# Perceiver block: the small attention steps between the products of the tail are regrouped

## What is computed

```
x = x + cross_attention(layernorm(x), ctx, ...)     # 32 heads of 128, 8 key heads
x = x + self_attention(layernorm(x), Wq, Wk, Wv, Wo)  # 32 heads of 32, 8 key heads, rope, causal
x = x + mix(layernorm(x), W_res, W_pre, W_post, ...)  # 4 streams, 50 Sinkhorn rounds, branch product
```

## Time and profile before

| what | value |
|---|---|
| median of 3 runs | 1107.49 us |
| the three runs | 1107.48, 1107.49 and 1110.83 us |
| profiled execution | span 1105.4 us; no other time of its own is given |
| PE busy | 1074.2 us (97% of the span) |
| DVE busy | 812.7 us (74%) |
| ACT busy | 482.0 us (44%) |
| POOL busy | 198.3 us (18%) |

### The profile page before, as it was taken

One profiled execution on the slowest core, in us unless ns is written; L12 is line 12 of the kernel. 1 busy time (PEld: TensorE's weight loads), 2 busy tenths in 40 slices (PEclk: granted clock), 3 DMA queues, 4 the chain that ended last, 5 costly groups with the idle time before them and its releaser, 6 DMA issues.

```text
span 1105.4 us, 17806 instructions
## 1 busy us (share of the span) xinstructions
PE 1074.2 (97%) x6380; PEld 902.4 (82%) x6380; DVE 812.7 (74%) x1942; ACT 482.0 (44%) x1033; POOL 198.3 (18%) x198
## 2 busy tenths in 40 slices
PE   6999999999999999999999999999999999999688
PEld 4888888788888888888888888888888878888467
DVE  5887667666667878776668877757536798758997
ACT  4544434444445446544444455434213334431417
POOL 2000000233223233333232230000001032140001
PEclk9999999999999999999999999999999999999889
DMA  9975775244543333244455312699935614000001
GB/s 238 174 200 126 159 161 146 51 110 110 114 99 87 76 76 70 62 94 109 97 107 114 76 34 58 136 215 242 213 63 105 109 24 76 2 14 1 1 1 77
DMA packets 184542, 111.29 MB, mean 101 GB/s; under 512 B 108040, under 2 KB 174472, under 8 KB 184480
## 3 DMA queue, kind: packets, MB, share of 16 engines
q1 hardware_dynamic: 182080, 109.17, 45.8%
q10 hardware_dynamic: 2400, 1.31, 0.5%
HBM read 90.98 MB, written 18.94 MB: 99 GB/s over the span
## 4 chain that ended last, share of the span: by engine, by line
PE 94%; DVE 3%; ACT 1%; DMA 1%; issue 0%; SPq 0%; DVEq 0%
PE ps L635 32%; PE ps L535 16%; PE ps L602 14%; PE ps L983 9%; PE ps L519 4%; PE ps L663 4%; PE ps L646 4%; PE ps L971 2%; PE ps L746 1%; PE ps L936 1%; DMA raw<-in_L_xattn_q_proj_w 1%; PE ps L879 1%; PE ps L1076 1%; PE ps L864 1%; PE ps L847 1%; PE ps L943 0%
## 5 line engine op out<-in xcount | busy, mean ns | idle before, releaser
L635 PE MATMUL ps<-wt,act 128*128 128x512 f32 x1536 | 381.0, 394 | 0.0
L635 PEld LDWEIGHTS ps<-wt,act 128*128 128x128 f32 x1536 | 278.1, 188 | 51.8 <-issue 0.4
L535 PE MATMUL ps<-wt,act 128*128 128x512 f32 x768 | 179.1, 394 | 1.4 <-ACT act L1109 1.0
L535 PEld LDWEIGHTS ps<-wt,act 128*128 128x128 f32 x768 | 145.0, 190 | 33.3 <-ACT wt L1114 3.4
L602 PE MATMUL ps<-act,wt 128*128 128x512 f32 x672 | 153.7, 390 | 0.0
L1114 ACT ACTIVATE wt<-raw 128x512 fp32r<-128x512 f32 x192 | 106.6, 625 | 95.6 <-PE ps L535 52.1
L602 PEld LDWEIGHTS ps<-act,wt 128*128 128x128 f32 x672 | 125.9, 188 | 26.0
L1565 DVE STREAM_TRANSPOSE raw<-raw 128x1024 f32<-128x1024 f32 x92 | 107.9, 1216 | 22.6 <-DMA raw<-in_L_xattn_o_proj_w 22.6
L983 PE MATMUL ps<-wt,act 128*128 128x512 f32 x480 | 121.5, 400 | 0.0
L1573 DVE TENSOR_TENSOR wt<-raw,wt 128x512 fp32r<-128x512 f32 x172 | 107.4, 682 | 15.9 <-ACT wt L1114 15.8
L2391 POOL TENSOR_TENSOR small<-small 128x4 f32<-128x4 f32 (+2 forms) x64 | 69.0, 1080 | 246.1 <-DVE small L1587 200.2
(11 more groups left out here) (178 smaller groups left out, 1274.4 us busy)
## 6 DMA issues: line engine op xcount, KB each, us to landing
xr<-in_ctx SPq DMA_DIRECT2D x64, 256.0 KB, 4.9
raw<-in_L_xattn_o_proj_w SPq DMA_DIRECT2D x32, 512.0 KB, 14.6
raw<-in_L_xattn_q_proj_w SPq DMA_DIRECT2D x28, 512.0 KB, 9.2
xr<-q_rows SPq DMA_DIRECT2D x16, 512.0 KB, 4.2
ot_hi<-spare SPq DMA_DIRECT2D x64, 128.0 KB, 2.0
act<-ot_hi SPq DMA_DIRECT2D x32, 256.0 KB, 9.4
q_rows<-G SPq DMA_DIRECT2D x28, 256.0 KB, 2.7
raw<-in_L_xattn_k_proj_w SPq DMA_DIRECT2D x8, 512.0 KB, 6.9
```

The lines of the kernel that those rows point to most:

```text
L535: mm = pe.matmul(banks[t], lhs(p == 2, c, t), wt[:, n_slot, int(p == 1), c, :], start=(acc_from and q == 0), stop=(acc_to and q == 3 * NC ...
L635: mm = pe.matmul(bank, src[int(p == 2)][:, c, kt * P:(kt + 1) * P], wt[:, slot, int(p == 1), c, :], start=(q == 0), stop=(q == 3 * NC - 1))
```

## The change

`scores2(b-1)`, `weigh2(b-3)` and `turn_probs2(b-2)` now stand in this order at the end of the block. The probabilities are turned into the upper halves of banks 2 to 5, beside the scores, no longer into banks 6 and 7. `turn_out2` moves to the next block, behind q = 8, and with it scale_out2, hi_out2 and lo_out2 go one block later. In the output projection the low activation parts of chunks 4 to 7 come last (`low_late`). ACT makes hi_out2 ahead of the weights' high parts, and copy_query ahead of exp2. DVE does scale_out2, rotate_query and lo_out2 ahead of read, peak and centre. `w24` lies in G[:, 0:1024] and is loaded when the last scores are made; `wb` keeps its place in the order of loads behind the last weighing, with a semaphore of its own. The copy of `w24T` moves to the front of ACT's block 11, and turn_rows(0, 1) from q = 11 to q = 17 of block 11.

```diff
-        w24 = G[:, 4096:5120]
+        w24 = G[:, 0:1024]
...
-            sp.wait_ge(o2_done, 8)
-            sp.dma_start(wb, w_branch.rearrange("(c p) n -> p c n", p=P)).then_inc(w24_loaded, 16)
+            sp.wait_ge(s2_done, 8)
             for a, n, w in ((0, 16, w_res), (16, 4, w_pre), (20, 4, w_post)):
                 sp.dma_start(w24[a:a + n, :], w).then_inc(w24_loaded, 16)
+            sp.wait_ge(o2_done, 8)
+            sp.dma_start(wb, w_branch.rearrange("(c p) n -> p c n", p=P)).then_inc(wb_loaded, 16)
...
-                if some(k - 1):
-                    pe.wait_ge(o2_scaled, k - 1)
+                if some(k - 2):
+                    pe.wait_ge(o2_scaled, k - 2)
...
                 pe.wait_ge(p2_exp, k + 1)
                 for half in range(2):
-                    if half == 0:
-                        pe.wait_ge(qt_read, min(k + 2, 8))
-                        if k:
-                            pe.wait_ge(o2_scaled, k)
-                    elif k:
-                        pe.wait_ge(o2_lo, k)
                     for j in range(4):
                         h, mg = 2 * half + j // 2, j % 2
-                        tr = pe.transpose(ps[:, 6 + half, j * P:(j + 1) * P],
+                        tr = pe.transpose(ps[:, 2 + h, 256 + mg * P:256 + (mg + 1) * P],
...
+                if k:
+                    pe.wait_ge(o2_lo, k)
                 pe.wait_ge(p2_copied, 2 * k + 2)
...
+            low_late = ([(c, p) for c in range(4) for p in range(3)] + [(c, p) for c in range(4, NC) for p in (0, 1)]
+                        + [(c, 2) for c in range(4, NC)])
...
-                    c, p = divmod(q, 3)
+                    c, p = low_late[q] if n >= 23 else divmod(q, 3)
                     if t == 0 and p == 0:
                         pe.wait_ge(w_lo, NC * n + c + 1)
+                    if n >= 23 and (c, p) == (4, 0):
+                        pe.wait_ge(o2_hi, 5 + t)
+                    if n >= 23 and (c, p) == (4, 2):
+                        pe.wait_ge(o2_lo, 5 + t)
...
-                    pe.wait_ge(o2_lo, 5 + t)
+                    pe.wait_ge(o2_lo, 1 + t)
...
                 def at_5():
-                    if 3 <= b <= 10:
-                        weigh2(b - 3)
...
+                def at_8():
+                    if 4 <= b <= 11:
+                        turn_out2(b - 4)
...
                     elif b == 11:
                         turn_rows(0, 0)
-                        turn_rows(0, 1)
...
                 def at_17():
-                    if 3 <= b <= 10:
-                        turn_out2(b - 3)
                     if 1 <= b <= 8:
                         turn_query(b - 1)
                     if b == 11:
+                        turn_rows(0, 1)
                         turn_rows(1, 0)
                         logits(0)
...
+                if 1 <= b <= 8:
+                    scores2(b - 1)
+                if 3 <= b <= 10:
+                    weigh2(b - 3)
                 if 2 <= b <= 9:
                     turn_probs2(b - 2)
-                if 1 <= b <= 8:
-                    scores2(b - 1)
...
             for b in range(1, 12):
                 if 3 <= b <= 10:
                     copy_probs2(b - 3)
+                if b == 11:
+                    sc.wait_ge(w24_turned, 1)
+                    sc.activation(w24T, ps[:, 3, 0:192].rearrange("p (c n) -> p c n", c=NC), ACT.Copy).then_inc(w24_ready, 1)
+                if 4 <= b <= 11:
+                    hi_out2(b - 4)
                 if b in later:
...
+                if b <= 8:
+                    copy_query(b - 1)
                 if 2 <= b <= 9:
                     exp2(b - 2)
-                if 3 <= b <= 10:
-                    hi_out2(b - 3)
-                if b <= 8:
-                    copy_query(b - 1)
...
                 v.wait_ge(s2_done, k + 1)
+                if k:
+                    v.wait_ge(p2_copied, 2 * k)
...
             for b in range(1, 12):
+                if b >= 4:
+                    scale_out2(b - 4)
                 if b <= 8:
                     rotate_query(b - 1)
...
+                if b >= 4:
+                    lo_out2(b - 4)
                 if 2 <= b <= 9:
                     read_scores2(b - 2)
                     peak_scores2(b - 2)
-                if 3 <= b <= 10:
-                    scale_out2(b - 3)
-                if 2 <= b <= 9:
                     centre_scores2(b - 2)
                 if b in turns:
                     for j in turns[b][1]:
                         turn_unit(turns[b][0], j)
-                if 3 <= b <= 10:
-                    lo_out2(b - 3)
```

More of the change, by code:

```diff
@@ L210, in perceiver @@
         w24_loaded, w24_turned, w24_ready = sem("w24_loaded"), sem("w24_turned"), sem("w24_ready")
+        wb_loaded = sem("wb_loaded")
         f_done, f_ready, lg_done, lg_read, xp_done, xp_read, y_done, y_read = (sem(n) for n in (
@@ L897, in turn_rows @@
                     pe.wait_ge(f_ready, same_bank)
+                elif half == 0:
+                    pe.wait_ge(o2_scaled, 8)
                 else:
@@ L938, in branch @@
                 mm.then_inc(xp_done, 1)
+                if t == 0:
+                    pe.wait_ge(wb_loaded, 16)
                 pe.wait_ge(xp_read, t + 1)
@@ L974, in mix, with tile_products @@
                         mm.then_inc(mix_done, 1)
-            def tile_products(n, t, at_11, at_17, at_5=None, bank=None):
+            low_late = ([(c, p) for c in range(4) for p in range(3)] + [(c, p) for c in range(4, NC) for p in (0, 1)]
+                        + [(c, 2) for c in range(4, NC)])
+            def tile_products(n, t, at, bank=None):
                 for q in range(3 * NC):
-                    c, p = divmod(q, 3)
+                    c, p = low_late[q] if n >= 23 else divmod(q, 3)
                     if t == 0 and p == 0:
                         pe.wait_ge(w_lo, NC * n + c + 1)
+                    if n >= 23 and (c, p) == (4, 0):
+                        pe.wait_ge(o2_hi, 5 + t)
+                    if n >= 23 and (c, p) == (4, 2):
+                        pe.wait_ge(o2_lo, 5 + t)
                     k = c * UW + t * P
@@ L984, in tile_products @@
                                    start=(q == 0), stop=(q == 3 * NC - 1))
[L985 to L990, removed]
+                    if q in at:
+                        at[q]()
                 mm.then_inc(acc_done, 1)
@@ L1000, in key_at_11 @@
                     turn_key(t - 2)
-                tile_products(20, t, key_at_11 if t >= 2 else None, None)
+                tile_products(20, t, {11: key_at_11} if t >= 2 else {})
                 if t < 2:
@@ L1042, in at_17 @@
                     if b == 11:
+                        turn_rows(0, 1)
                         turn_rows(1, 0)
                         logits(0)
-                tile_products(n, t, at_11, at_17, at_5, b % 2)
+                tile_products(n, t, {5: at_5, 8: at_8, 11: at_11, 17: at_17}, b % 2)
                 if b == 0:
                     turn_key(3)
+                if 1 <= b <= 8:
+                    scores2(b - 1)
+                if 3 <= b <= 10:
+                    weigh2(b - 3)
                 if 2 <= b <= 9:
                     turn_probs2(b - 2)
-                if 1 <= b <= 8:
-                    scores2(b - 1)
                 if b == 10:
-                    pe.wait_ge(w24_loaded, 64)
+                    pe.wait_ge(w24_loaded, 48)
                     pe.wait_ge(s2_read, 8)
@@ L1397, in copy_probs2 @@
                     sc.wait_ge(p2_turned, 2 * k + half + 1)
-                    sc.activation(pT2[:, 2 * half:2 * half + 2, :, :].rearrange("p h m n -> p (h m) n"),
-                                  four(ps[:, 6 + half, :]), ACT.Copy).then_inc(p2_copied, 1)
+                    sc.activation(pT2[:, 2 * half:2 * half + 2, :, :].rearrange("p h m n -> p h (m n)"),
+                                  ps[:, 2 + 2 * half:4 + 2 * half, 256:512], ACT.Copy).then_inc(p2_copied, 1)
             def hi_out2(k):
@@ L1419, in _ @@
                         hi_w(n, n % 2, c, raw_slot(n))
+                if b <= 8:
+                    copy_query(b - 1)
                 if 2 <= b <= 9:
                     exp2(b - 2)
-                if 3 <= b <= 10:
-                    hi_out2(b - 3)
-                if b <= 8:
-                    copy_query(b - 1)
-            sc.wait_ge(w24_turned, 1)
-            sc.activation(w24T, ps[:, 3, 0:192].rearrange("p (c n) -> p c n", c=NC), ACT.Copy).then_inc(w24_ready, 1)
             sc.wait_ge(const_loaded, 144)
```

## The result

The changed kernel took 1116.41 us (median of 4 runs, 1115.07 to 1119.47) against 1107.89 us for the kernel before on the same chip: ratio 1.0077, 95% interval 1.0063 to 1.0091. Slower, as forecast, by 8.5 us where 5.5 were forecast. Measured twice more beside the experiments the ratio was 1.0069 (1.0055 to 1.0083) and 1.0074 (1.0057 to 1.0091). The profiled execution of the changed kernel took 1117.38 us with a span of 1115.6. All ratios are of fast runs; one of ten executions of the second experiment took 1221.15 us at a mean granted clock of 0.841 and is in no ratio.

What follows compares the result with a forecast made beforehand. PE, 94% of the chain, was taken to bound the kernel up to tile 1's logits; 4.57 us by block 11's start plus 0.90 in block 11 made 5.5 us, on a median of 1107.49 giving 1113.0 us; range 1108.3 to 1116.5.

Steps and rivals of the forecast that it cites:

- What bounds the kernel: Whole kernel: PE holds 94% of the chain; the change is worth the shift of tile 1's logits.
- from there the same work: Behind the logits of tile 1: work stays the same, so the 5.5 us later logits are the whole loss.
- Seams and block 2: PE's full block without waits takes 9.45 us, 0.29 less; block 2's stall of 1.35 us goes.
- The exponent's wait: Blocks 4 to 8: PE waits 0.37 us ahead of the turns of probabilities; a block lasts 9.82, not 9.45.
- the wait for the high part: Blocks 8 and 9: high part ready at 3.5, wanted at 3.28; 0.2 us, inside the later wait for the exponent.
- Block 9: POOL's third low part overlaps DVE's centring and delays it by 1.0 us; the block lasts 10.82.
- Block 10: PE waits for POOL's low parts of unit 24, chunks 4 to 7: 12.29 us; the wait alone costs 4.5.
- rival 4: Block 10: PE's clock falls from 2.4 to 1.2 GHz, so 3.15 us of work takes twice as long: 1116.2 us; 12%.
- Block 11: Output turn of group 7, 0.44 us, and a wait of 0.46 for the second half's turn: 0.90 in all.
- Range: Total time 1108.3 to 1116.5 us: the low end takes in rivals 2 and 3, the high end rival 4.
- the forecast's own range: Total time 1111 to 1115 us, from centring's delay, hand-overs and POOL's start; the forecast itself had 63%.
- rivals 1 to 3: Only PE's seams count: 1104.0, 8%; only block 10's wait fails: 1108.5, 8%; only the exponent's wait fails: 1108.7, 9%.

Runs made afterwards that it cites:

- the second experiment: Changed kernel with DVE's lo_out2 moved behind the centring (blocks 4 to 7) or behind the peak (blocks 8 and 9): 1111.59 us, ratio 1.0031.
- the two mended versions: Changed kernel with ACT's and DVE's old orders put back, 1107.37 us; the same with four edits more, 1104.91 us.
- the three with fillers: Changed kernel with unused identity matmuls in PE's waits: 34 in block 10, 1119.76 us; fewer, in blocks 9 and 10, 1115.24 and again 1113.28 us.
- the first experiment: Changed kernel with ACT making the weights' high parts ahead of hi_out2 again in blocks 9 and 10: 1110.37 us, ratio 1.0024.
- block 9 alone: Changed kernel with ACT making the weights' high parts ahead of the output's in block 9 only: 1115.83 us, measured once.

## Why the prediction was right, and what it missed

- **What bounds the kernel.** Right in seven of the thirteen profiles: what the logits of tile 1 lost or gained is what the kernel lost or gained there. In the second and third profiles and in the two mended versions the rest was 110.6 to 110.7 us, before 110.6. But "from there the same work" did not always take the same time. The rest was 113.4 in the first profile and in the second experiment's, 112.4 in two of the three with fillers, and 111.5 and 111.6 in those of the first experiment and of block 9 alone. The sum had no term for this.
- **Seams and block 2.** Right. Block 3, without a wait, took 9.03 (forecast 9.01), block 2 7.98 (forecast 7.93), and the stall went, as the timeline shows:

```profile
904.57 1.06 PE L849 MATMUL ps<-G,raw 32*64 32x64 f32 x64
905.57 1.09 PE L860 MATMUL ps<-ident,raw 128*128 128x128 f32 x8
906.41 4.37 PE L992 MATMUL ps<-wt,act 128*128 128x512 f32 x18
```

  In single records of block 3, the last of the scores (913.387) stands 0.147 ahead of the first of the weighing (913.534), as much as ahead of a large matmul in the kernel before (926.616 and 926.763), while two scores stand 0.016 apart: the seam between two tile sizes is not free. The Trainium skill, "TensorEngine Tiling (Array Packing)", Key Properties, says that a change of tiling mode drains TensorE. The 0.147 agrees with that. A block without waits is 9.50 rather than 9.45, because eight turns behind the weighing take 0.85, not 0.80.
- **The exponent's wait.** Right for blocks 4 to 7: 9.82 forecast, 9.83 measured, and lo_out2's place was the cause (second experiment). That the number is so close is partly luck: the work took 0.05 more than forecast, the wait 0.04 less (0.33 against 0.37). In block 8 it was the wait for the high part that counted, forecast at 0.2 and inside the exponent's wait, measured at 0.3 and with no wait for the exponent behind it.
- **Block 9.** Right at 10.82 against 10.83, with the centring at 2.20 (forecast 1.23 + 1.0). The Trainium skill, "SBUF — State Buffer", SBUF: two separate sides, has the port that DVE and POOL share as an exclusive lock. The 2.20 and POOL's 5.97 here, against 1.22 and 5.02 without an overlap, agree with that.
- **Block 10.** The mechanism was right: POOL's four chunks, with holes of 1.86, 0.49, 0.49 and 0.35 us ahead of PE's matmuls (forecast for PE's weight loads near 2 and three near 0.8; they idled 2.29 and three times 0.93); the time was short by 1.15 us in one profile, 1.7 and 1.5 in the others. This is the step that failed: "holes here are at most 2 us, and no row shows a fall after so short ones", on which rival 4 got 12%. The same text had just worked out a hole of 2.5 us in block 9. And holes of less than 2 us were no protection either: in the first profile the clock held through that hole and fell in block 10, behind a hole of 1.86, and so it did in the second experiment and in the one on block 9, where no hole was longer. In all three profiles of the changed kernel the clock fell, in two of them twice. Rival 4's price, 3.15 us, was too dear, since the clock was back at the upper level before the block ended (mean 0.99 from 987 to 990 in the first profile): the falls cost 1.3 us to the logits in the first profile, 2.6 and 2.5 in the others (of that 0.8 in block 9). But it belonged into the forecast, since it follows from the forecast's own waits. Without the falls (fillers) the logits came at 105.43 and 105.53, where the sum said 105.3.
- **Block 11.** 0.90 forecast, 0.98 measured, with the wait where it was put:

```profile
994.03 1.03 PE L901 MATMUL ps<-ident,xr 128*128 128x128 f32 x8
995.32 1.97 PE L923 MATMUL ps<-G,raw 128*128 128x24 f32 x16 [0.25 <-ACT raw L1444]
```

  Moving that turn three matmuls forward brought the block to 11.30.
- **Range.** 1108.3 to 1116.5 held 1116.41 just barely, and with luck: the forecast's own range, 1111 to 1115, did not hold it, and the upper end had been set for rival 4, at a price that did not come; falls of the clock in blocks 9 and 10 (1.3 to 2.6 us) and, in some executions, behind the logits (2.8 in one profile) filled it instead. The rivals of the other side did not come: rivals 1 to 3 each needed a wait not to come that queue order forces.

## What to carry to other kernels

Grouping small matmuls saves its 0.23 us a block only if whoever feeds them is not moved behind a slower wait: follow each moved step through every queue that it enters, and ask what now stands behind its wait (here weights behind an output turn in ACT's queue, scores behind an output copy in DVE's). And when a sum gives a stream of matmuls holes of 2 us, put the clock's fall into the forecast, not among the rivals. In blocks 9 and 10 of this case it fell in all six profiles whose longest hole was 1.86 to 2.47 us, and in none of the seven others, whose longest hole there was 1.44; what lies between was not tried.

## What the runs showed of the hardware

- PE's clock fell from 2.4 to 1.2 GHz toward the end of a hole of 2.5 us (in the second profile at 974.5, the hole from some 972.2 to 974.69), and at 983.6 in the first profile, where the longest hole of the last 9 us was 1.9. In the second experiment, with no hole longer than 1.86 in blocks 9 and 10, it fell at 979.5. I had expected none of this.
- The same fall can land behind the logits. There PE runs 18 matmuls of 256 columns as fillers (L1083). In the first profile of the changed kernel, and in the second, they read:

```profile
1077.04 10.76 PE L1083 MATMUL ps<-G,ident 128*128 128x256 f32 x36 [3.32 <-DVE small L2158]
```

```profile
1078.33 8.01 PE L1083 MATMUL ps<-G,ident 128*128 128x256 f32 x36 [3.25 <-DVE small L2158]
```

  The mean granted clock is 0.74 from 1077.0 to 1087.6 in the first; there, partly at the lower level, they take 2.75 us more and push the mix back: this is the 113.4 in the table against 110.6. The same line took 10.79 us in the second experiment, and 9.69 and 9.70 in two runs with fillers. It differs between executions of one kernel, and with it some 3 us of its time; why it lands there in one and not in the other is open.
- A matmul of the identity by 128 columns of the identity took 0.22 us in two records; a transpose of the same size takes 0.11.
